# Folding the feed-forward weights inside the last head group of a fused attention and feed-forward kernel

## The reference

```python
x = x + _layernorm(_L0_attn_ref(_layernorm(x), ...))       # 16 query heads, 8 key heads of 128, causal,
                                                           # p = softmax(q1 k1) - lam * softmax(q2 k2), o = p v, rms norm, @ out_w.T
x = x + _layernorm(_L0_ffn_ref(_layernorm(x), ...))
# _L0_ffn_ref:
x = fwht(x * SU_ug) / SCALE                                # over 256 channels
x_up   = x @ W_up.T   * (Wscale_ug[:INTER] * SCALE)        # INTER = 1024
x_gate = x @ W_gate.T * (Wscale_ug[INTER:] * SCALE)
x = silu(x_gate) * x_up
x = fwht(x * SU_dp) / SCALE                                # over 1024 channels
x = x @ W_down.T * (Wscale_dp * SCALE)
```

## Time and profile before

| | us |
|---|---|
| span of the profiled execution | 1448.5 |
| time of that execution | 1450.26 |
| median of three runs | 1446.94 |
| TensorE busy | 1376.5 (95%) |
| VectorE, ScalarE, GpSimd busy | 1049.2, 873.5, 841.6 |
| mean granted TensorE clock | 0.981 |

### The profile page before, as it was taken

The page is one execution under the profiler, slowest core; times in us unless marked ns, Lnnn a source line. Parts: engine busy times, 40 slices in busy tenths (PEclk is TensorE's granted clock), DMA queues, the critical chain, the costliest instruction groups (busy, mean ns, idle before and its releaser), DMA issues. The chain is left out here.

```text
span 1448.5 us, 26445 instructions
## 1 busy us (share of the span) xinstructions
PE 1376.5 (95%) x8344; PEld 1217.6 (84%) x8344; DVE 1049.2 (72%) x2644; ACT 873.5 (60%) x2465; POOL 841.6 (58%) x1316
## 2 busy tenths in 40 slices
PE   4989999999999999999999999999999999569998
PEld 3879999988989999889899998898999998547887
DVE  6667778776677777767777787677777877576654
ACT  2466766666666666665676666666666666353331
POOL 1357666664766666656666656556766666334444
PEclk9989999999999999999999999999999999879999
DMA  3000000000000000000000000000000000310000
GB/s 127 1 30 1 1 2 1 1 16 1 1 30 2 1 1 2 15 1 1 30 1 1 2 1 1 16 1 1 1 1 1 1 1 1 86 60 1 12 15 33
DMA packets 14407, 18.36 MB, mean 13 GB/s; under 512 B 4416, under 2 KB 12736, under 8 KB 13760
## 3 DMA queue, kind: packets, MB, share of 16 engines
q1 hardware_dynamic: 13712, 15.35, 3.3%
q10 hardware_dynamic: 560, 1.32, 0.2%
HBM read 14.58 MB, written 2.10 MB: 12 GB/s over the span
## 5 line engine op out<-in xcount | busy, mean ns | idle before, releaser
L543 ACT ACTIVATE e<-score_bank,negmx 128x512 f32<-128x512 f32 (+2 forms) x640 | 393.7, 625 | 75.6 <-DVE negmx L652 75.0
L806 POOL TENSOR_TENSOR e<-e,e 128x512 f32<-128x512 f32 (+3 forms) x256 | 294.3, 1150 | 21.3
L648 DVE TENSOR_REDUCE mx<-score_bank 128x1 f32<-128x512 f32 (+1 forms) x384 | 244.1, 636 | 26.4 <-PE score_bank L448 25.5
L446 PE MATMUL score_bank<-k_hi,q_hi 128*128 128x512 f32 (+2 forms) x640 | 253.2, 396 | 4.7 <-ACT e L543 3.0
L468 PE MATMUL turn_bank<-v_hl,pT_hi 128*128 128x512 f32 x679 | 251.7, 405 | 5.2 <-DVE pT_lo L658 5.2
L789 POOL TENSOR_TENSOR inv_s<-s,neg_one 128x1 f32<-128x1 f32 x128 | 70.3, 549 | 318.8 <-DVE s L773 318.1
L448 PE MATMUL score_bank<-k_hi,q_lo 128*128 128x512 f32 (+2 forms) x640 | 232.4, 363 | 0.0
L447 PE MATMUL score_bank<-k_lo,q_hi 128*128 128x512 f32 (+2 forms) x640 | 231.5, 362 | 0.0
L470 PE MATMUL turn_bank<-v_hl,pT_lo 128*128 128x256 f32 x679 | 190.7, 281 | 0.0
L803 POOL TENSOR_SCALAR e<-e,ratio 128x512 f32<-128x512 f32 (+3 forms) x256 | 176.4, 689 | 12.0
L643 DVE CUSTOM_DVE_ANT_0 score_bank<-score_bank,mask 128x384 f32<-128x384 f32 (+3 forms) x256 | 143.0, 559 | 55.6 <-PE score_bank L448 54.5
(11 more groups left out here) (266 smaller groups left out, 3535.7 us busy)
## 6 DMA issues: line engine op xcount, KB each, us to landing
w_raw<-in_w_qkv_dram SPq DMA_DIRECT2D x3, 1024.0 KB, 4.7
w_raw<-in_w_o_dram SPq DMA_DIRECT2D x4, 512.0 KB, 3.3
out_dram<-d_out SPq DMA_DIRECT2D x16, 128.0 KB, 1.7
x_in<-in_hidden_dram SPq DMA_DIRECT2D x3, 512.0 KB, 8.4
x_res<-in_hidden_dram SPq DMA_DIRECT2D x1, 1536.0 KB, 13.3
w_raw<-in_w_qkv_dram ACTq DMA_DIRECT2D x1, 1024.0 KB, 6.8
raw<-in_w_up_dram SPq DMA_DIRECT2D x2, 512.0 KB, 5.3
raw<-in_w_gate_dram SPq DMA_DIRECT2D x2, 512.0 KB, 7.8
```

Source lines behind the costliest of these rows:

```text
L446: pe.matmul(bank[:, 0:w], qh, kh, start=True, stop=False)
L543: act.activation(e, S[k % NS][:, 0:w], ACT.Exp, bias=negmx[:, d % 2, m, s:s + 1], accum_out=ssum[:, d % 4, s, m, c:c + 1]).then_inc(s_act, 1)
L648: dve.tensor_reduce(mx[:, d % 2, m, s, c:c + 1], S[k % NS][:, 0:w], X, ALU.max)\
L806: pool.tensor_tensor(a, a, b, ALU.add).then_inc(p_pool, 1)
```

## The change

The three blocks become one, and the feed-forward part becomes further steps of the same list.

- The host transposes the gate, up and down weights, so the 48 turns of them on TensorE are gone. The row scales of gate and up are no longer multiplied into the weights: they are given to the Silu and to the product behind it as columns. What is loaded goes into `w_raw`, free after the last group's weights are split, and into `e1`.
- The fold is made of new steps. `FH` n: GpSimd adds or subtracts the two halves of a raw weight (the 256-point transform's last stage, n below 8), ScalarE and VectorE split the result. `F` n: two products with the Hadamard matrix, then scaling and splitting. `HAD` grows the Hadamard matrix on GpSimd. `DB` n are the butterflies of the down weights, 8 on GpSimd and 8 on VectorE, now of 512 elements each.
- In the last group the pairs go in `LAST_ORDER`, from the outside in, so that tiles 0, 1, 14 and 15 (chunk 0 of the feed-forward part) are done after two pairs, and chunk 1 after four. The norms (`N`) and turns (`Z`) of chunks 0 and 1 stand in halves 13 to 15 and 22 to 24 of the last group, `FH` and `F` 0 to 7 in halves 16, 17, 20, 21 and 28 to 31, `HAD` at the end of half 5.
- In the drain, gate (`G`) and up (`U`) products of chunk 0 are put between the steps of `LAST_HALVES`. The split of the product (`HH`) follows one gate product later. The norms of chunks 2 and 3, the butterflies, and `F` 8 to 11 are hung behind certain up products (`with_gated`).

```diff
+LAST_ORDER = (0, 7, 1, 6, 2, 5, 3, 4)
...
+LAST_GROUP = {5: 'TSTSSOSTPSoQTPPTPH',
+              13: 'TSTNSSONSTPSoQNTPPTP', 14: 'TSSNTSSTPNTSoQNTPPPTO', 15: 'TSTNSSONSTPSoQNTPPTPN',
+              16: 'TSSTfSSTPfTSoQTPPPTO', 17: 'TSTfSSOSTPSfoQTPPTP',
+              20: 'TSSTfSSTPfTSoQTPPPTO', 21: 'TSTfSSOSTPSfoQTPPTP',
+              22: 'TSSNTSSTPNTSoQNTPPPTO', 23: 'TSTNSSONSTPSoQNTPPTP', 24: 'TSSNTSSTPNTSoQNTPPPTNO',
+              28: 'TSSTfSSTPfTSoQTPPPTO', 29: 'TSTfSSOSTPSfoQTPPTP',
+              30: 'TSSTfSSTPfTSoQTPPPTO', 31: 'TSTfSSOSTPSfoQTPPTP'}
+LAST_HALVES = ('ToTPTToOPUU', 'UTUTOTPUPTPO', 'TUoTUTTOUoPUo')
...
+def chunk_tiles(c):
+    return (2 * c, 2 * c + 1, TILES - 2 - 2 * c, TILES - 1 - 2 * c)
+def pair_of(u):
+    return (LAST_ORDER if u // (DUOS // 2) == GROUPS - 1 else PAIR_ORDER)[u % (DUOS // 2)]
...
+    def fold_steps(n):
+        return [("FH", n), ("FH", n + 1), ("F", n), ("F", n + 1)]
     keys, values = [], []
+    norms = [x for c in range(2) for x in norm_steps(c, range(4)) + turn_steps(c)]
+    folds = [x for n in range(0, 8, 2) for x in fold_steps(n)]
+    hadamard = [("HAD", None)]
+    gated = [0]
+    with_gated = {
+        3: norm_steps(2, (0,)), 4: norm_steps(2, (1,)) + [("DB", 0), ("DB", 1)],
+        5: norm_steps(2, (2,)) + [("DB", 2), ("DB", 3)], 6: norm_steps(2, (3,)) + [("DB", 4), ("DB", 5)],
+        7: turn_steps(2) + [("DB", 6), ("DB", 7)], 8: [("DB", 8), ("DB", 9)], 9: [("DB", 10), ("DB", 11)],
+        10: [("DB", i) for i in range(12, 16)], 11: [("FH", 8), ("FH", 9)],
+        12: [("F", 8), ("F", 9), ("FH", 10), ("FH", 11)], 13: [("F", 10), ("F", 11)],
+        16: norm_steps(3, (0,)), 17: norm_steps(3, (1,)), 18: norm_steps(3, (2,)), 19: norm_steps(3, (3,)),
+        22: turn_steps(3)}
+    def emit_gated():
+        k, up = divmod(gated[0], 2)
+        gated[0] += 1
+        emit("U" if up else "G", k)
+        if not up and k > 0:
+            emit("HH", k - 1)
+        if up:
+            for what in with_gated.get(k, ()):
+                emit(*what)
...
+    assert not (exps_due or factors_due or mixes_due or norms or folds)
+    while to_turn or to_project:
+        if to_turn:
+            emit("OT", to_turn.pop(0))
+        emit_gated()
+        if to_project:
+            emit("OP", to_project.pop(0))
+    for c in range(FFN_CHUNKS):
+        while gated[0] < 2 * JT * (c + 1):
+            emit_gated()
+        if c + 1 == FFN_CHUNKS:
+            emit("HH", JT * FFN_CHUNKS - 1)
+        if c > 0:
+            for n in range(QB * (c - 1), QB * c):
+                emit("DN", n)
+    for n in range(QB * (FFN_CHUNKS - 1), QB * FFN_CHUNKS):
+        emit("DN", n)
+    emit("DEND", None)
...
+            def wug(f, co):
+                return ((k_hi[:, co, 3 * BANK:], k_lo[:, co, 3 * BANK:]),
+                        (v_hl[:, 12 + co, :], v_hl[:, 14 + co, :]),
+                        (wq_hi[:, co, :], wq_lo[:, co, :]),
+                        (v_hl[:, 10 + co, :], w3_lo[:, co, :]))[f]
+            wd_hl = v_hl[:, 0:JT, :]
+            wd_a, wd_b = e1[:, 0:4, :], e1[:, 5:9, :]
...
+                sp.wait_ge(w_lo, w_use["WO", (GROUPS - 1, 1)] + 1)
+                for f in range(2):
+                    sp.dma_start(raw_w(f), w_ug[f]).then_inc(raw_landed[f], 16)
+                sp.wait_ge(kv_dve, last_value_split + 1)
+                load_input(0)
+                sp.wait_ge(t_full, t_use["Z", (0, 1)] + 1)
+                load_input(1)
+                sp.wait_ge(folded_ready, 2)
+                sp.dma_start(raw_w(2), w_ug[2]).then_inc(raw_landed[2], 16)
+                sp.wait_ge(folded_ready, 4)
+                sp.dma_start(raw_w(3), w_ug[3]).then_inc(raw_landed[3], 16)
+                sp.wait_ge(t_full, t_use["Z", (1, 1)] + 1)
+                load_input(2)
+                sp.wait_ge(t_full, last_turn[CHUNKS * (ALL_DUOS - 1) - 1] + 1)
+                sp.dma_start(wd_a, w_d.rearrange("p (q n) -> p q n", q=4)).then_inc(wd_landed, 16)
+                sp.wait_ge(t_full, t_use["Z", (2, 1)] + 1)
+                load_input(3)
...
+                    elif kind == "F":
+                        if what == 0:
+                            pe.wait_ge(had_ready, 1)
+                        pe.wait_ge(wt_lo_ready, what + 1)
+                        bank = free_bank(kind, what)
+                        pe.matmul(bank[:, :], had[:, :], wt_hi[:, what % 2, :], start=True, stop=False)
+                        pe.matmul(bank[:, :], had[:, :], wt_lo[:, what % 2, :], start=False, stop=True)\
+                          .then_inc(t_full, 1)
...
+                        if what < 2:
+                            pe.wait_ge(s_act, last_score - (last_score - b) % NS + 1)
+                        else:
+                            pe.wait_ge(h_ready if up else g_act, what - 1)
...
+                    elif kind == "FH":
+                        if what == 0:
+                            act.wait_ge(kv_full, last_value_split + 1)
+                        if what >= 2:
+                            act.wait_ge(t_full, t_use["F", what - 2] + 1)
+                        if what < 8:
+                            act.wait_ge(folded_ready, what + 1)
+                            source = folded[:, what % 2, :]
+                        else:
+                            act.wait_ge(wd_dve, 8)
+                            source = wd_b[:, what - 8, :]
+                        act.activation(wt_hi[:, what % 2, :], source, ACT.Copy).then_inc(wt_hi_ready, 1)
...
+                    elif kind == "DB" and what >= 8:
+                        dve.wait_ge(wd_pool, 8 if what % 4 >= 2 or what >= 12 else 6)
+                        if what >= 12:
+                            dve.wait_ge(wd_dve, 4)
+                        source, to = (wd_b, wd_a) if what < 12 else (wd_a, wd_b)
+                        first, step, op = (what % 4 // 2 * 2, 1, what % 2) if what < 12 else (what % 2, 2, what % 4 // 2)
+                        dve.tensor_tensor(to[:, first + step * op, :], source[:, first, :], source[:, first + step, :],
+                                          ALU.subtract if op else ALU.add).then_inc(wd_dve, 1)
+                    elif kind == "U":
+                        b, at = 2 * (what % 2) + 1, WS_COL + 2 * (what % JT) + 1
+                        dve.wait_ge(g_act, what + 1)
+                        dve.wait_ge(u_full, what + 1)
+                        if what == 0:
+                            dve.wait_ge(wt_lo_ready, 8)
+                        if what >= 2:
+                            dve.wait_ge(h_lo_ready, what - 1)
+                        dve.scalar_tensor_tensor(out=h_f[:, what % 2, :], in0=S[b][:, :], scalar=col[:, at:at + 1],
+                                                 in1=gate[:, what % 2, :], op0=ALU.mult, op1=ALU.mult)\
+                           .then_inc(h_ready, 1)
...
+                    elif kind == "HAD":
+                        pool.wait_ge(cols_landed, 16)
+                        pool.tensor_scalar(su_s[:, :], col[:, SU_COL:SU_COL + CT], float(HID) ** -0.5, 0.0,
+                                           ALU.mult, ALU.add).then_inc(scales_ready, 1)
+                        pool.tensor_scalar(sud_s[:, :], col[:, SUD_COL:SUD_COL + JT], float(INTER) ** -0.5, 0.0,
+                                           ALU.mult, ALU.add).then_inc(scales_ready, 1)
+                        pool.wait_ge(kv_act, kv_use["V", (GROUPS - 1, V_UNITS - 1)] + 1)
+                        pool.wait_ge(v_lo, GROUPS * V_UNITS)
+                        grown = ident[:, :]
+                        for stage in range(7):
+                            to = folded[:, stage % 2, 0:P] if stage < 6 else had[:, :]
+                            a = grown.rearrange("p (n two h) -> p n two h", two=2, h=1 << stage)
+                            b = to.rearrange("p (n two h) -> p n two h", two=2, h=1 << stage)
+                            pool.wait_ge(had_step, 2 * stage)
+                            pool.tensor_tensor(b[:, :, 0, :], a[:, :, 0, :], a[:, :, 1, :], ALU.add)\
+                                .then_inc(had_step, 1)
+                            ins = pool.tensor_tensor(b[:, :, 1, :], a[:, :, 0, :], a[:, :, 1, :], ALU.subtract)
+                            if stage < 6:
+                                ins.then_inc(had_step, 1)
+                            else:
+                                ins.then_inc(had_ready, 1)
+                            grown = to
...
+                    elif kind == "FH" and what < 8:
+                        f, co = divmod(what, CT)
+                        pool.wait_ge(raw_landed[f], 16)
+                        if what == 0:
+                            pool.wait_ge(had_ready, 1)
+                        if what >= 2:
+                            pool.wait_ge(wt_lo_ready, what - 1)
+                        pool.tensor_tensor(folded[:, co, :], raw_w(f)[:, 0, :], raw_w(f)[:, 1, :],
```

(21 more changed lines are left out.)

852 lines of the change are left out of this document (337 added, 515 removed).

## The result

| | kernel before | changed kernel |
|---|---|---|
| time, median of 4 runs each | 1447.58 us (1446.67 to 1449.44) | 1457.58 us (1455.23 to 1458.38) |
| ratio, 95% interval | | 1.0055 (1.0038 to 1.0072) |
| profiled execution, its span | 1448.5 us span | 1455.23 us, span 1453.1 |
| mean granted clock of TensorE | 0.981 | 0.982 |

A forecast was written before the change was run, and what follows sets the result against it. TensorE was taken to bound attention and feed-forward, everything else the stretch between. Work of 1400.0 us plus 8 of group stalls and 6 in drain and first chunk gave 1414 us of span, median 1412.5, range 1401 to 1428.

The forecast's parts named there:

- `FH` behind GpSimd: Last group: ScalarE waits for GpSimd's add queued behind mixing; 1 us for each of four pairs, 4 us.
- norms of chunks 0 and 1: Last group, VectorE: some 5 us come late, mostly absorbed; 1.5 us for each chunk, 3 us.
- `HAD`: Last group: 14 small GpSimd instructions, at most 7.7 us, with mixes queued behind; 1 us, bounds 0 and 4.
- pair order: Last group: the new order changes no amount of work; 0, within 2 us either way.
- drain and feed-forward: Drain and first chunk: turn 127 waits about 1.1 us, VectorE's butterflies delay `F` 8 by 5 us; 6 us together.
- The sum on TensorE: Whole kernel: the 46.2 us stretch leaves, drain holes fill, added products are paid in full; 1400.0 us if nothing stalls.
- The five terms of work: After the last scores: drain 25.2 us, holes -4.9, first chunk 22.5, `F` 8 to 11 1.9, rest 114.6.
- rivals 1 and 4: 1: all waits hide, stalls 0 to 6 us, chance 0.17. 4: the drain isn't filled, 1418 us, chance 0.04.
- Rival 5: Last group: ScalarE stands behind GpSimd's whole 6.5 us burst at each of eight `FH` steps, 1456.5 us median; chance 0.05.
- rival 3: Group and butterflies: VectorE and GpSimd block each other, about 9 us reach TensorE, 1421 us; chance 0.19.
- term of 5 us for this stretch: First chunk: VectorE's eight butterflies at pairs 8 to 10 make `FH` 8 and `F` 8 wait; bounds 0 and 12.
- What would show it: Profile signs: full clock from 40 us, `F` 8 late; wrong if ScalarE's group waits exceed 10 us or norm instructions double.

The follow-up runs named there:

- fold ahead: Changed kernel with GpSimd's add of each FH step issued earlier as its own step, at starts of odd halves (last in the middle of 29): 1433.51 us.
- order alone: Kernel before with only the pair order of the last group changed: 1450.41 us, ratio 0.9997.
- handoff alone: Kernel before with eight GpSimd-to-ScalarE handoffs added in halves 16, 20, 28 and 30, results unread: 1479.24 us, ratio 1.0189.
- narrow norms: Fold-ahead kernel with VectorE's norm instructions of chunks 0 and 1 cut to 8 of 256 columns: 1423.97 us.
- Narrow down weights: Fold-ahead kernel with all 16 `DB` steps cut to 8 columns of each piece: 1426.00 us.
- norms later: Changed kernel with chunk 2's norm moved from up products 3 to 6 to 10 to 13, its turn from 7 to 15: 1459.62 us.
- down weights later: Fold-ahead kernel with norms of chunks 0 and 1 spread over halves 13 to 27, plus the down weights' butterfly steps moved later: 1436.44 us.

## Why the prediction was wrong

Against the forecast span of 1414 us, 39.1 are missing (1453.1). By its own terms, the stalls of the group from fold ahead, order alone and the changed kernel:

| term | forecast (bounds) | measured |
|---|---|---|
| `FH` behind GpSimd | 4 (0 to 12) | 22.8 |
| norms of chunks 0 and 1 | 3 (0 to 10) | 13.9 |
| `HAD` | 1 (0 to 4) | 1.9 |
| pair order | 0 (-2 to 2) | 0.4 |
| other stalls of the group | none | 48.6 - 5.95 - 39.0 = 3.6 |
| drain and feed-forward | 6 (0 to 13) | 171.3 - 159.3 = 12.0 |
| start of the group, tail | 0 | -1.3, -0.3 |

**The sum on TensorE was right.** The 46.2 us left the path, the drain holes were filled, the tail is 6.2 us. The five terms of work give 159.3 us behind the last scores, and 171.3 were measured, 12.0 more. TensorE is busy for 160.3 of the 171.3 (the windows above), so nearly all of the 12.0 are idle time: 5.86 us before the turns of chunk 2, 2.7 in the gaps at 1378.01 and 1382.70 us, 2.4 in the drain. So rivals 1 and 4 are out.

**`FH` is the step that failed most.** The prediction read the burst of the earlier trace rows and set `FH` 0 some 4.5 us into the half, less 2 until ScalarE is there, less 3 us of cover. Four things were mis-sized in it. The 4.5 us are the end of the mix ahead of the add; the add's own 1.26 us were left out. The add ends 7.3 us into the half, since GpSimd's factor starts 2.9 us into it and not 0.8 as in the earlier trace rows: it waits 3.62 us for sums from VectorE. TensorE's cover is 2.2 us, not 3. And the price did not end with the gap: the four gaps sum to 17.7 us (4.07, 4.21, 4.53, 4.91) of 22.8. Behind them TensorE runs at a granted 0.50 for another 4.9, 5.4, 3.4 and 4.1 us (until 1117.54, 1161.92, 1243.84 and 1267.73), which costs it up to half of that, some 9 us; that is enough for the other 5.1, since halves 28 and 30 keep smaller stalls of their own with the fold ahead. The prediction priced no low clock in the group. The handoff alone puts the same 27 us of wait into the kernel before. There GpSimd's factor starts 0.8 us into half 16, as in the earlier trace rows, so the late factor is not needed for it:

```profile
1098.62 0.55 POOL L798 TENSOR_TENSOR inv_s<-s,neg_one 128x1 f32<-128x1 f32 x1
...
1103.89 2.48 POOL L859 TENSOR_TENSOR v_sum<-w_raw 128x512 f32<-128x512 f32 x2
```

Both adds of this half stand behind the whole burst, and the first (half of 2.48 us) ends 7.3 us into the half all the same. What the 1 us per pair left out was that a step in the middle of the list comes at the end of GpSimd's burst, and that the engines behind ScalarE have some 2 us, no more.

**Rival 5 named the mechanism**, with a burst of 6.5 us a step and a decision from 5.3 us. It costs 22.8 / 8 = 2.9 us a step; by itself it would have left the change a clear gain, as its point of decision says. It became slower with the norms and the drain on top. The bounds of the single terms were each drawn as if the cover were free for that term alone.

**The norms: from free time in the mean to none in the place.** "Within three halves that have 22% free" took the share of 25 halves for that of the three. With the norms in it VectorE is busy for 95% and 88% of halves 13 and 14, and the experiment with narrow norms says that a microsecond of it costs some 0.8. Of the 13.9 us the width carries 8.4 (up to 1.7 of it low clock in half 24) and the wait for GpSimd's root 2.2; what is left, some 3.3, wasn't separated and is hardly more than two traces differ by. It is not the adds of `FP` in halves 13 and 15, which take the same in the changed kernel without them (8.53 and 10.77 us). The prediction had in the earlier trace rows a row that priced this: 47 us of new work "would stall for over 20", and set it aside because the pieces are short. The group stalled for 42.6.

**VectorE and GpSimd blocking each other (rival 3)** is there at two places. In the group most of the norm's instructions kept to 0.35 to 0.49 us, as was named, and the four that make the z of chunk 0 took 0.40 to 0.41 us each. The four of chunk 1, in half 24, did not; a mean of 609 ns, as in the lines above, hides it. The instructions of that line (shortest, median and longest in ns), then the timelines of VectorE, GpSimd and TensorE in the changed kernel:

```profile
L1173 DVE TENSOR_SCALAR bv<-acc,n_mv,n_rs x4: 402/702/1444, 1197.0 to 1201.2; 128x256 f32<-128x256 f32 x4
```
```profile
1197.02 2.16 DVE L1173 TENSOR_SCALAR bv<-acc,n_mv,n_rs 128x256 f32<-128x256 f32 x2
...
1200.63 0.93 DVE L1173 TENSOR_SCALAR bv<-acc,n_mv,n_rs 128x256 f32<-128x256 f32 x2
```
```profile
1196.41 1.26 POOL L1245 TENSOR_SCALAR e<-e,ratio 128x512 f32<-128x512 f32 x1
1197.75 1.28 POOL L1248 TENSOR_TENSOR e<-e,e 128x512 f32<-128x512 f32 x1
```
```profile
1201.62 0.66 PE L757 MATMUL turn_bank<-ident,bv 128*128 128x128 f32 x4 [2.84 <-DVE bv L1173]
```

The four took 0.80, 1.44, 0.61 and 0.40 us beside GpSimd's mix, 1.6 us more than four at 0.40. TensorE stood 2.84 us for them, and from 1202.88 to 1206.29 us its granted clock was 0.50. So a part of the norms' 13.9 us is rival 3's. In the first chunk more instructions are long. The timelines of VectorE and GpSimd, where the earlier trace rows has the same instructions at some 0.5 us each:

```profile
1311.22 2.54 DVE L1163 SCALAR_TENSOR_TENSOR acc<-acc,n_rs,bv 128x256 f32<-128x256 f32 x2
...
1320.29 2.61 DVE L1173 TENSOR_SCALAR bv<-acc,n_mv,n_rs 128x256 f32<-128x256 f32 x2 [1.43 <-POOL n_rs L1328]
...
1323.48 1.96 DVE L1173 TENSOR_SCALAR bv<-acc,n_mv,n_rs 128x256 f32<-128x256 f32 x2
```
```profile
1310.77 2.72 POOL L1336 TENSOR_TENSOR e<-e,out_b_row 128x512 f32<-128x512 f32 x2
...
1320.22 2.53 POOL L1336 TENSOR_TENSOR e<-e,out_b_row 128x512 f32<-128x512 f32 x2
1322.71 1.31 POOL L1348 TENSOR_TENSOR k_lo<-v_sum,k_hi 128x512 fp32r<-128x512 f32 x1
1323.99 2.58 POOL L1341 TENSOR_TENSOR e<-e 128x512 f32<-128x512 f32 x2
```
```profile
1325.50 1.11 PE L757 MATMUL turn_bank<-ident,bv 128*128 128x128 f32 x4 [5.86 <-DVE bv L1173]
```

Two VectorE instructions take 2.61 us where two of the earlier trace rows take 1.05, and they end at 1322.90 where GpSimd's pair ends at 1322.75; the next two take 1.96. That makes the z of chunk 2 late, and TensorE stands 5.86 us before its turn, then has its low clock again (products 0.43 us apart from 1327.69). Narrow down weights take most of it away. That run takes away the blocking and the work together, and moving the steps (norms later, down weights later) only moved the stall, so no run shows how much of this price is the blocking and how much the sum of the two engines' work. The Trainium skill ("SBUF — State Buffer", section "SBUF: two separate sides") says that of a GpSimd instruction and a VectorE instruction with two SBUF inputs or in a two-port mode, whichever starts first holds the shared port pair for its whole instruction and the other fully blocks. By this rule, the trace agrees: the pair of VectorE's starts 0.07 us behind GpSimd's and ends 0.15 us after it. These have one SBUF tensor each, beside their per-partition scalars, so they would have to be in a two-port mode, which no run shows. The prediction's term of 5 us for this stretch, inside bounds of 0 to 12, had the right engines and the wrong step: it expected `F` 8 to be late, and the turns of chunk 2 were.

**What would show it**, as it was named: ScalarE's waits for GpSimd in the group were over 10 us (26.7); three of the norms' 40 wide instructions of chunks 0 and 1 were long in the group, one at over three times its 0.40 us (1.44); the clock fell in the first chunk (0.89 from 1300.8 to 1332.3), and also five times in the group, in halves 16, 20, 24, 28 and 30. A clock that is full from 40 us on was in neither kernel (0.50 from 75.8 to 85.9 us before, from 76.5 to 83.3 after).

## What to carry to other kernels

An engine that waits in its own order for another engine's queue stops all that stands behind it: put the producer's instruction at least a half ahead of the consumer's, at a place where the producer is idle. Here that alone turned a loss of 10 us into a gain of 1.1%, and 1.5% (1426 us) with two more steps moved. Before work goes into a "full" loop, read the free time of each engine in the very iterations that get it; a share over the whole loop says nothing of them. And don't give every new wait the same cover: what TensorE has queued is spent once.

## What the runs showed of the hardware

- TensorE's granted clock was at the lower level (0.50) for 4.40 us after a single idle stretch of 4.07 us in half 16. After gaps of 1.1 and 1.6 us in the feed-forward part (1378.01 and 1382.70 us) the window from 1378 to 1390 us shows 1.00. In between the same gap went both ways: behind one of 2.84 us in half 24 of the changed kernel it fell to 0.50, and behind one of 2.81 us at the same place with narrow down weights it stayed at 1.00 (1184.5 to 1196 us).
- GpSimd's instructions of `HAD`, unchanged in their work, cost 1.9 us at the end of half 5 and nothing at the start of half 9.
- On VectorE, the instruction with two per-partition scalars takes at shortest 271 ns for 8 columns (narrow norms) and 399 ns for 256 (fold ahead), and at longest 1242 and 1447 ns; the one with a single scalar takes 225 to 232 and 347 to 354 ns.
